# Reordering the dense turns of an attention and expert kernel: transposed probabilities copied first on VectorE, scores issued at the slots' ends, an output bias added ahead on GpSimd

## Time and profile before

| what | value |
|---|---|
| median of 3 runs | 1257.14 us (1256.35 to 1259.25) |
| profiled execution, its own time | 1254.63 us |
| its span, first to last instruction | 1252.8 us |
| busy shares of the span | PE 87%, DVE 70%, ACT 67%, POOL 52% |
| chain that ended last, by engine | PE 28%, DVE 28%, ACT 21%, issue 15% |
| dense turns, from about 86 us to 604 us | 518 us |
| one mid turn, by its first transpose (411.34 to 476.20 us) | 64.86 us, PE busy 57.86 us |
| expert stage and final sum | 649 us |

### The profile page before, as it was taken

One profiled execution on the slowest core, in us unless ns is written; L12 is line 12 of the kernel. 1 busy time (PEld: TensorE's weight loads), 2 busy tenths in 40 slices (PEclk: granted clock), 3 DMA queues, 4 the chain that ended last, 5 costly groups with the idle time before them and its releaser, 6 DMA issues.

```text
span 1252.8 us, 30088 instructions
## 1 busy us (share of the span) xinstructions
PE 1091.6 (87%) x9070; PEld 1009.1 (81%) x9070; DVE 882.5 (70%) x2032; ACT 842.5 (67%) x1987; POOL 654.7 (52%) x910
## 2 busy tenths in 40 slices
PE   3887889899888889898799999999999999999950
PEld 3866677777777777776799999999999999999950
DVE  7567655656565656566688888888888888888825
ACT  2455767667666767676577777787777878877720
POOL 6002543323241506052267777777777777777740
PEclk9789999999999999999999999999999999999985
DMA  8870011010101010131331111125411240125119
GB/s 290 268 241 22 35 36 39 34 38 34 38 34 38 34 38 30 36 124 39 126 135 31 38 36 36 34 88 197 145 28 40 88 147 28 34 88 200 44 56 348
DMA packets 68338, 106.72 MB, mean 85 GB/s; under 512 B 7693, under 2 KB 60046, under 8 KB 66640
## 3 DMA queue, kind: packets, MB, share of 16 engines
q1 hardware_dynamic: 60704, 86.55, 21.4%
q0 software_dynamic: 7600, 19.74, 4.5%
HBM read 138.52 MB, written 37.50 MB: 141 GB/s over the span
## 4 chain that ended last, share of the span: by engine, by line
PE 28%; DVE 28%; ACT 21%; issue 15%; DMA 3%; DVEq 1%; SPq 1%; POOL 1%; ACTq 0%; POOLq 0%
PE bank L1207 7%; PE bank L1209 6%; PE bank L1208 6%; ACT hf L798 6%; DVE gu_s L1126 5%; DVE sm L979 5%; DVE gu_s L1133 5%; ACT gs L791 3%; DVE hf L1146 3%; PE bank L1294 3%; PE bank L1325 2%; ACT gu_s L809 2%; DVE ys L1162 2%; ACT ht L802 2%; ACT dw_s L816 2%
## 5 line engine op out<-in xcount | busy, mean ns | idle before, releaser
L1207 PE MATMUL bank<-xt_h,gu_s 128*128 128x256 f32 (+1 forms) x1014 | 292.4, 288 | 23.5 <-DVE hf L1146 21.0
L1208 PE MATMUL bank<-xt_l,gu_s 128*128 128x256 f32 (+1 forms) x1014 | 286.7, 283 | 0.0
L1209 PE MATMUL bank<-xt_h,gu_s 128*128 128x256 f32 (+1 forms) x1014 | 286.2, 282 | 0.0
L620 POOL TENSOR_TENSOR ht<-hf,ht 128x256 fp32r<-128x256 f32 (+1 forms) x273 | 242.7, 901 | 63.5 <-ACT ht L802 53.7
L1133 DVE TENSOR_TENSOR gu_s<-raw_gu,gu_s 128x512 fp32r<-128x512 f32 (+1 forms) x273 | 204.1, 770 | 64.0 <-ACT gu_s L809 63.9
L1207 PEld LDWEIGHTS bank<-xt_h,gu_s 128*128 128x128 f32 (+1 forms) x1014 | 191.3, 189 | 30.6 <-issue 26.6
L1209 PEld LDWEIGHTS bank<-xt_h,gu_s 128*128 128x128 f32 (+1 forms) x1014 | 191.4, 189 | 0.0
L1208 PEld LDWEIGHTS bank<-xt_l,gu_s 128*128 128x128 f32 (+1 forms) x1014 | 191.0, 188 | 0.0
L798 ACT ACTIVATE hf<-hf 128x256 f32<-128x256 f32 (+1 forms) x273 | 113.5, 416 | 85.8 <-DVE hf L1146 81.2
L611 POOL TENSOR_TENSOR dw_s<-raw_dw,dw_s 128x256 fp32r<-128x256 f32 x117 | 109.4, 961 | 67.6 <-ACT dw_s L816 67.1
L1207 PE MATMUL bank<-dw_s,ht 128*128 128x256 f32 x468 | 133.3, 285 | 2.7 <-issue 2.7
(11 more groups left out here) (177 smaller groups left out, 2779.5 us busy)
## 6 DMA issues: line engine op xcount, KB each, us to landing
raw_gu<-in_gu_dram SPq DMA_DIRECT2D x39, 1648.0 KB
raw_dw<-in_dw_dram SPq DMA_DIRECT2D x39, 768.0 KB
xs_dram<-zrec SPq DMA_DIRECT2D x6, 1677.0 KB, 14.5
xr<-xs_dram SPq DMA_DIRECT2D x39, 258.0 KB, 2.7
yg<-y_dram SPq DMA_DIRECT2D x16, 512.0 KB, 8.3
xwin<-xn_dram SPq DMA_DIRECT2D x8, 640.0 KB, 4.9
raw_dw<-in_dw_dram SPq DMA_DIRECT2D x78, 64.0 KB
xg<-in_x_dram SPq DMA_DIRECT2D x8, 512.0 KB, 6.2
```

Source lines behind the costliest of these rows:

```text
L620: nc.gpsimd.tensor_tensor(low, hf[0:m, ring(c), :], ht[0:m, p, 0, c, :].bitcast(F32), ALU.subtract).then_inc(h_split, 1)
L1207: nc.tensor.matmul(dst, lhs[0], rhs[0], start=start, stop=False)
L1208: nc.tensor.matmul(dst, lhs[0], rhs[1], start=False, stop=False)
L1209: return nc.tensor.matmul(dst, lhs[1], rhs[0], start=False, stop=stop)
```

## The change

VectorE's slot now begins with `pt_copy`, then `add_attention`, one head group of `masked_min`, `share_of`, and the other three groups. The last of the eight `gelu_lo` is moved behind the next turn's first `pt_copy`. `k_copy` 1 is moved ahead of `attention_stats`. The addition of `bo_b` to `x2` (L1011) is gone from VectorE: GpSimd computes `xb = xn + bo_b` for a whole turn (`add_bias`) behind the `residual` of the turn before, for the first turn inside its slot computation, and `add_attention` adds `xb` instead of `xn`, with a wait for all four of the turn. TensorE issues the scores of tiles 2 and 3 at the ends of slots 0 and 1, and those of tile 5 between `turn_x2` 0 and 1. V4 is computed ahead of Y3 instead of behind it, which exchanges their banks, and ScalarE copies V4 ahead of the square root.

```diff
-         "A2", "V2", "O3", "V3", "A3", "Y3", "V4", "X0", "X1"] + [f"F{c}" for c in range(FC1)])
+         "A2", "V2", "O3", "V3", "A3", "V4", "Y3", "X0", "X1"] + [f"F{c}" for c in range(FC1)])
...
+            def add_bias(g):
+                for j in range(GT):
+                    nc.gpsimd.tensor_tensor(xb[:, j, :], one(xn[:, ds(g * GT + j, 1), :]), bo_b, ALU.add).then_inc(xb_ready, 1)
...
+            pool.wait_ge(bo_ready, 1)
+            add_bias(0)
             pool.wait_ge(starts_ready, 1)
...
-            with pool.Fori(0, NG) as g:
+            with pool.Fori(0, NG - 1) as g:
                 scatter(g)
                 residual(g)
+                settle(pool)
+                add_bias(g + 1)
+            scatter(NG - 1)
+            residual(NG - 1)
...
+                if more:
+                    v_copy(at, 4)
                 act.wait_ge(ln_stats, g * GT + GT)
                 nc.scalar.activation(sd2[:, :], mv2[:, :, 1], ACT.Sqrt, bias=eps).then_inc(ln_sd, 1)
-                if more:
-                    v_copy(at, 4)
...
                 bk, free = full(f"A{j}", at)
-                nc.vector.tensor_tensor(x2[:, j, :], bk[:, 0:D], one(xn[:, ds(at.g * GT + j, 1), :]), ALU.add).then_inc(free, 1)
+                dve.wait_ge(xb_ready, at.g * GT + GT)
+                nc.vector.tensor_tensor(x2[:, j, :], bk[:, 0:D], xb[:, j, :], ALU.add).then_inc(free, 1)
...
-                nc.vector.tensor_tensor(x2[:, j, :], x2[:, j, :], bo_b, ALU.add).then_inc(pre_ready, 1)
-                dve.wait_ge(pre_ready, n)
...
-                    if ahead:
-                        masked_min(at, j + 1, (0, 1), mask)
-                    share_of(at, j)
                     pt_copy(g, j)
+                    if j == 0 and at.seg != "first":
+                        gelu_lo(at.f, FC1 - 1)
                     if j:
                         add_attention(at, j - 1)
                     if ahead:
-                        masked_min(at, j + 1, (2, 3), mask)
+                        masked_min(at, j + 1, (0,), mask)
+                    share_of(at, j)
+                    if ahead:
+                        masked_min(at, j + 1, (1, 2, 3), mask)
                     if more and j == 2:
                         k_copy(at, 0)
+                        k_copy(at, 1)
                     if j:
                         attention_stats(at, j - 1)
-                    if more and j == 2:
-                        k_copy(at, 1)
...
-                gelu_lo(g)
+                for c in range(FC1 - 1):
+                    gelu_lo(g, c)
...
-                    if j != 2 and (more or j == 1 or j == 0):
-                        scores(at, j + 2)
...
+                scores(at, 2)
                 begin_slot(1)
...
+                scores(at, 3)
                 begin_slot(2)
...
-                fill(3, *range(FC1))
                 if more:
                     values(at, 4)
+                fill(3, *range(FC1))
                 turn_x2(at, 0)
+                if more:
+                    scores(at, GT + 1)
                 turn_x2(at, 1)
```

More of the change, by code:

```diff
@@ L213, in program @@
         x2 = tile("x2", [GT, D])
+        xb = tile("xb", [GT, D])
         st2, mv2, sd2, rs2 = tile("st2", [GT, 6]), tile("mv2", [GT, 2]), tile("sd2", [GT]), tile("rs2", [GT])
@@ L257, in program @@
         nbq_ready, probs_ready, share_kept, share_ready = sems("nbq_ready probs_ready share_kept share_ready")
-        pre_ready, ln6, ln_stats, ln_sd, ln_rstd, scaled, x2_ready, x2_half, x2_summed = sems(
-            "pre_ready ln6 ln_stats ln_sd ln_rstd scaled x2_ready x2_half x2_summed")
+        bo_ready, xb_ready, ln6, ln_stats, ln_sd, ln_rstd, scaled, x2_ready, x2_half, x2_summed = sems(
+            "bo_ready xb_ready ln6 ln_stats ln_sd ln_rstd scaled x2_ready x2_half x2_summed")
         gelu_hi, gelu_split = sems("gelu_hi gelu_split")
@@ L970, in add_bv @@
                 nc.vector.tensor_tensor(bo_b, bk[:, 0:D], bo_b, ALU.add).then_inc(free, 1)
+                b, n = m_use("BO", at)
+                dve.wait_ge(free, n + 1)
+                dve.sem_inc(bo_ready, 1)
             def masked_min(at, j, pairs, mask):
@@ L1032, in x2_lo, with gelu_lo @@
                 nc.vector.tensor_tensor(x2t_l[:, :, cs], bk[:, :].rearrange("p (k c) -> p k c", k=KC), x2t_h[:, :, cs].bitcast(F32), ALU.subtract).then_inc(free, 1)
[L1034 to L1037, removed]
+            def gelu_lo(g, c):
+                dve.wait_ge(gelu_hi, g * FC1 + (c + 1))
+                nc.vector.tensor_tensor(h_l[:, c, :], h1[:, c % 2, :], h_h[:, c, :].bitcast(F32), ALU.subtract).then_inc(gelu_split, 1)
             def dense_sum(at, j):
@@ L1109, in turn @@
                 x2_lo(at, 1)
-                gelu_lo(g)
+                for c in range(FC1 - 1):
+                    gelu_lo(g, c)
             turns_of(dve, turn)
+            gelu_lo(NG - 1, FC1 - 1)
             for j in range(GT):
```

## The result

| | before | after |
|---|---|---|
| median of 7 runs, us | 1257.36 (1252.46 to 1259.9) | 1250.4 (1246.48 to 1253.78) |
| profiled execution, us | 1254.63 | 1246.48 |
| its span, us | 1252.8 | 1244.6 |
| mean granted clock | 0.969 | 0.953 |

The ratio is 0.9941, with a 95% interval of 0.9919 to 0.9962: faster by 0.6%, where 1246 was forecast. The time is inside the range, 4.4 us above the forecast. Of all runs in this document one, of e10, fell into a slow state (1385.55 us at a granted clock of 0.753), and the ratios leave it out.

The account below looks back on a forecast made before the run. TensorE was taken to set the pace, a gain being only its idle time, about 7 us a turn. Six mid turns -9.9, first turn +1.3, last -2.3 gave -11 us: 1246 us against the median, range 1238 to 1253.

Parts of the forecast that it names:

- no clock time is at stake: Dense turns: the granted clock reads 1.00 in the mid turn, so the change has no clock time to win or lose.
- Slot 0: Mid turn: copy wait -1.17 and wait ahead of scores -0.50 go, ScalarE's late group 2 copy adds 0.46; -1.2 us.
- Slot 1: Mid turn: copy and mask waits of 0.8 each go, a new 0.8 wait for the shares comes; -0.9 us.
- Slot 2: Mid turn: shares 0.1 earlier, `k_copy` 1 removes a 0.68 wait, `normalise` holds the next k unit 0.36; -0.5 us.
- Slot 3 and X: Mid turn: later exponentials put out_project 0.69 later, Y3 fills X0's wait, F0's second half comes later; +0.7 us.
- The border with GpSimd: Between turns: GpSimd's additions stretch `gelu_lo` 7, delaying masks and exponentials by 0 to 1.07 us; taken as +0.25.
- The mid turn: Sum of the four slots and the GpSimd contention: -1.65 us a turn, -9.9 for six.
- The bias: Slot 3's chain to X0: taking the 0.46 us addition off VectorE counted at nothing, ScalarE's table load coming later.
- First turn: Scores moved behind window transposes +1.1, additions +0.7 in slot 1, slot 3 +0.7, earlier -0.9; taken +1.3, bounds 0 to +3.
- Last turn: Gains of slots 0 and 1 (-2.1) and 0.5 from the removed bias; -2.3 us after contention.
- Rival 1: Mid turns: exponentials might not hold the shares, so more waits go, 1 us a turn more; 1239 us, chance 0.20.
- Rivals 2 to 4: GpSimd and VectorE fully exclude each other: 1252, chance 0.15; nothing to measure: 1257, 0.06; exponentials become the bound: 1264, 0.07.

Follow-up runs that it names:

- e10: Changed kernel with first masks ahead of `add_attention`, output bias back on VectorE, and `attention_stats` behind `normalise`, `window_lo` and `k_copy` 2 and 3: 1237.61 us, ratio 0.9841.
- e13: Changed kernel with `k_copy` 1 behind `attention_stats` again, as before the change: 1250.3 us, ratio 0.9947.
- e2: Changed kernel with the output bias added by VectorE again and GpSimd's additions gone: 1259.04 us, ratio 1.0005.
- e12: e11 with ScalarE's copy of V4 behind the square root in the first turn only: 1228.15 us, ratio 0.9767.
- e11: e1 with `attention_stats` moved behind `normalise`, `window_lo` and `k_copy` 2 and 3: 1233.55 us, ratio 0.9814.
- e1: Changed kernel with VectorE's masks of head group 0 ahead of `add_attention`, directly behind `pt_copy`: 1230.45 us, ratio 0.9772.
- e4: Changed kernel with head group 3's transposes in slot 3 issued three times instead of once, except in the last turn: 1243.89 us, ratio 0.989.
- e8: Changed kernel with `share_of` ahead of the first masks, which puts them 0.45 us later: 1271.18 us, ratio 1.0096.

## Why the prediction was right in the time, and where its steps were not

- **What bounds it.** TensorE, as said: every difference above is a wait of TensorE, or its clock. The sentence that no clock time is at stake was the step that failed. It read the clock of before as a property of the stage; it depends on how long TensorE stands still, and the change lengthened slot 3's wait. Four mid intervals lose 1.3 us each (5.2 us), the last turn some 1.3 behind the waits of its slot 2. The prediction had the masks of slot 3 late, but not the wait of 1.22 and 1.03 us that this leaves TensorE with: it lists waits of 0.5 to 0.8 in slots 0 and 1 only.
- **Slot 0:** -1.2 forecast, -1.40 measured (13.09 to 11.69). The shares go 5.06 us after the slot's start, exactly as worked out.
- **Slot 1:** -0.9 forecast (its own terms, -0.8, -0.8 and +0.8, sum to -0.8), -0.74 measured; shares at +4.85 for +4.82.
- **Slot 2:** -0.5 forecast, -0.59 measured; shares at +4.77 for +4.83. The part of it put on `k_copy` 1 was wrong: e13 shows that the move gives nothing.
- **Slot 3 and X:** +0.7 forecast, made of -0.14 up to X0 and +0.83 from X0 to F0's second half. Measured: -0.44 (13.39 to 12.95) and +0.87 (2.95 to 3.82), together +0.4. I had the shares 0.12 and out_project 0.3 too late. The new wait of 0.63 between F0's halves was foreseen as 0.8; X0 doesn't wait, as foreseen; Y3, forecast to wait 0.3, doesn't either.
- **The border with GpSimd:** +0.25 forecast. The four additions take longer than the 0.73 assumed, their median is 1184 ns, and `gelu_lo`'s median went from 694 to 827 ns (754 without the additions, in e2). The first exponential still comes 3.43 us after the slot's start, the same as before: in the mid turns it cost nothing that reached TensorE. The changed kernel, GpSimd's timeline, then lines L548 and L1048 (duration ns min/median/max):

```profile
406.13 4.24 POOL L548 TENSOR_TENSOR xb<-xn,rowb 128x256 f32<-128x256 f32 x4
```

```profile
L548 POOL TENSOR_TENSOR xb<-xn,rowb x32: 723/1184/1257, 97.3 to 535.8; 128x256 f32<-128x256 f32 x32
L1048 DVE TENSOR_TENSOR h_l<-h,h_h x64: 676/827/1262, 144.5 to 586.9; 128x512 fp32r<-128x512 f32 x64
```

- **The mid turn:** 64.86 to 63.2 was forecast, and a turn without a fall takes 62.7. Six times -2.15 would have been -12.9. The falls gave back 5.2, and a fall in the first interval of before (67.49, 2.6 over the others), which is gone, took off 2.6: that makes the -10.19 measured. Only 1.7 of the 2.6 lie between X0 and slot 0, where that fall is (138 to 142 us); the rest is in slot 0 (14.05, 12.8 to 13.5 in the others) and was not looked into. The -9.9 forecast came close by luck: two terms that it did not have, +5.2 and -2.6, and turns that gained 0.5 more than it said nearly cancel.
- **The bias:** the sum had it "at nothing". By e2 it is worth 1.2 us a turn (contention included), since `normalise` and `dense_sum` stand behind it. The forecast slot lengths held nonetheless, because they were set by the exponentials, with the bias already taken out of VectorE's order; only the price put on the part was wrong.
- **First turn:** +1.3 forecast with 0 to +3 as bounds; from the first scores to the first X0 it went from 57.27 to 60.20, +2.9. By slots it is +3.1 in slot 0, +0.7, -3.0, and +2.2 from slot 3 to X0 (14.22 against 12.06). Of these 2.2, the wait ahead of X0 is 0.5 (2.91, and 2.38 before); no Y3 covers ScalarE's copy and table load there, and e12 takes 0.8 off by its order. Slot 3 has the waits of the mid turns, 1.31 and 1.06, and a fall behind them (from 130 us); before had no fall there, and e11, with a wait of 0.58 and no fall, takes 12.31 there. The forecast's own terms (1.1, 0.7, 0.7 and -0.9) sum to 1.6, and the additions of GpSimd, done at 100.1 us, delayed nothing: `add_attention` 0 went at 101.12 when out_project was done. What the 3.1 of slot 0 are made of was not looked into.
- **Last turn:** -2.3 forecast, +0.85 measured from the seventh X0 to the eighth. I carried slot 1's gain over from the mid turn; here it went from 8.62 to 8.70, as it had hardly had those waits. Only slot 0 gained (1.11). X to slot 0 took 0.97 more, and slots 2 and 3, across whose border the fall lies, 0.91 more.
- **The rivals.** Rival 1 had the right direction for the mid turns (0.5 more gone, half of its 1 us), but not by its mechanism: the exponentials do hold the shares, to 0.06 us as worked out in slots 0 to 2, and the 0.5 comes from slot 0, from slot 3 with X, and from the border with GpSimd. Rivals 2 to 4 did not come. None of them was a rival about the clock.

The span of the profiled execution fell by 8.2 us where 11 were forecast. The 2.8 missing are 1.6 in the first turn and 3.2 in the last, less 0.3 in the mid intervals and 1.9 in the stages that the change doesn't touch (0.62 ahead of the first scores, 1.25 in the expert stage); that is 2.6, and rounding is the rest. The rest of the 4.4 is that the median lies 3.9 above the profiled execution, where I had allowed 2.5.

## What to carry to other kernels

When a wait is removed, ask what the next one will be and which engine's order sets it. Here the shares waited for exponentials that waited for masks that stood behind an addition, and the swap of two calls (e1) gave three times what the change gave. Cost an instruction that is taken off an in-order engine by everything queued behind it, not by the one chain that it belongs to. A pause of TensorE must be priced with the clock it may lose: look at the granted clock behind the longest pauses. Remove such a pause if an order can do it (e1, ratio 0.9772), and fill it, if need be with repeated work, if not (e4, 0.989).

## What was unexpected of the hardware

- **Pauses and the clock.** Waits of 1.22 and 1.02 us with 0.44 us of work between them, inside a turn in which TensorE is over 90% busy (58.18 of 62.64 us), are followed by 3 to 4 us at a granted clock of 0.50 in four of six intervals. With 0.35 and 1.02 it is none of six (e4), with 1.71 and 1.03 six of six (e8), three of them twice as long. One such fall costs 1.3 us, a long one 2.6. Why it comes in four and not in six no run shows.
- **Additions side by side.** GpSimd's addition of 128x256 takes 723 ns at least and 1184 at the median, where VectorE runs `gelu_lo` beside it. The Trainium skill's "SBUF — State Buffer", section "SBUF: two separate sides", has the two engines exclude each other for such operations, and the trace agrees, with both engines' maxima (1257 and 1262 ns) far over their minima. Two of VectorE's masks, with one operand in a PSUM bank, ran beside the additions of 406.13 to 410.37 (at 409.69 and 410.04) and kept their 0.42 us.
- **Table load and order.** ScalarE's table load starts right behind the activation ahead of it, here V4's copy, which ends at 453.14, and the root right behind the load. So the place of one neighbouring copy moves the load. In the mid turns that was hidden; in the first turn, e12's 0.8 us. ScalarE of the changed kernel, mid turn:

```profile
453.17 1.28 ACT L786 ACT_TABLE_LOAD   x1
454.46 0.30 ACT L786 ACTIVATE sd<-mv,cst 128x4 f32<-128x4 f32 x1
```
